# Last weight block cut 448+64 instead of 384+64x2, its wide store issued by ScalarE, engine programs run in two visits

## The reference

```python
fl = _ln(xf, pn_g, pn_b)
pf = _merge(attention(fl, Wqk_p, Wv_p) + conv) @ Wout_p
wv = _heads(_ln(xw, wn_g, wn_b) @ Wv_w)      # [4, 16384] @ [16384, 1024]
wf = nds @ wv + conv(wv)
wf = _merge(wf) @ Wout_w                     # [4, 1024] @ [1024, 16384]
out = wfeat + wf                             # back to the image
return out + x
```

## Time and profile before

| | us |
|---|---|
| median of 3 runs | 747.84 |
| the profiled execution's own time | 747.63 |
| its span, first to last instruction | 746.40 |
| around the span | 1.23 |
| DMA queue 1 busy | 99.5% of 16 engines' span |
| PE busy (matmul) | 436.4, 58% |
| DVE, ACT, POOL busy | 91.5, 38.2, 9.3 |
| granted TensorE clock, mean | 0.78 |

### The profile page before, as it was taken

The page is one execution under the profiler, slowest core; times in us unless marked ns, Lnnn a source line. Parts: engine busy times, 40 slices in busy tenths (PEclk is TensorE's granted clock), DMA queues, the critical chain, the costliest instruction groups (busy, mean ns, idle before and its releaser), DMA issues.

```text
span 746.4 us, 6667 instructions
## 1 busy us (share of the span) xinstructions
PE 436.4 (58%) x2895; PEld 129.9 (17%) x2895; DVE 91.5 (12%) x254; ACT 38.2 (5%) x80; POOL 9.3 (1%) x21
## 2 busy tenths in 40 slices
PE   7699944444445454454586989445444454544548
PEld 5333200000001111111122332000000011111113
DVE  2765200000002000000005161000000020000000
ACT  2211100000000000000001111000000000000000
POOL 2100000000000000000001000000000000000000
PEclk9689977777767777777788899876776777777779
DMA  9999999999999999999999999999999999999998
GB/s 394 447 394 436 454 415 439 436 443 418 436 446 418 439 433 443 421 432 446 418 439 436 417 434 443 446 418 432 443 432 432 432 446 418 432 443 432 432 415 347
DMA packets 7923, 320.45 MB, mean 429 GB/s; under 512 B 1049, under 2 KB 1585, under 8 KB 2153
## 3 DMA queue, kind: packets, MB, share of 16 engines
q1 hardware_dynamic: 7913, 320.31, 99.5%
HBM read 319.82 MB, written 0.49 MB: 429 GB/s over the span
## 4 chain that ended last, share of the span: by engine, by line
DMA 64%; PE 32%; DVE 3%; ACT 1%; issue 0%; SPq 0%; DVEq 0%; ACTq 0%
DMA ring<-halves 60%; PE bank L485 10%; PE bank L512 9%; PE bank L404 4%; DMA ring<-last 4%; PE bank L421 2%; PE bank L413 2%; PE bank L536 1%; PE bank L341 1%; PE bank L323 0%; PE bank L389 0%; DMA cst<-blurs 0%; DVE ring L722 0%; PE bank L381 0%; PE bank L354 0%
## 5 line engine op out<-in xcount | busy, mean ns | idle before, releaser
L485 PE MATMUL bank<-ring,stage 128*4 128x512 f32 x1024 | 141.4, 714 | 141.1 <-DMA ring<-halves 141.1
L512 PE MATMUL bank<-ring,wf_t 128*32 128x512 f32 x960 | 137.9, 739 | 127.3 <-DMA ring<-halves 127.3
L512 PEld LDWEIGHTS bank<-ring,wf_t 128*32 128x32 f32 x960 | 33.7, 133 | 221.1 <-DMA ring<-halves 121.0
L485 PEld LDWEIGHTS bank<-ring,stage 128*4 128x4 f32 x1024 | 27.0, 97 | 255.1 <-DMA ring<-halves 154.1
L932 DVE TENSOR_TENSOR image<-bank,image 128x32 f32 (+1 forms) x30 | 5.1, 193 | 277.6 <-PE bank L323 277.6
L897 DVE COPY wv_t<-bank 128x32 f32<-128x32 f32 x2 | 0.4, 192 | 287.1 <-PE bank L323 287.1
L323 PE MATMUL bank<-ident,area 128*128 128x128 f32 (+1 forms) x117 | 18.3, 284 | 12.3 <-ACT area L653 11.1
L653 ACT COPY area<-bank 128x512 f32<-128x512 f32 x15 | 8.8, 586 | 281.2 <-PE bank L512 281.2
L404 PE MATMUL bank<-extra,area 128*64 128x512 f32 x64 | 18.2, 734 | 3.3 <-DVE area L806 3.3
L469 PE MATMUL bank<-extra,area 128*64 128x512 f32 x64 | 17.6, 712 | 2.0 <-DVE area L871 2.0
L323 PEld LDWEIGHTS bank<-ident,area 128*128 128x128 f32 (+1 forms) x117 | 12.5, 141 | 30.9 <-ACT area L653 23.8
(11 more groups left out here) (208 smaller groups left out, 217.0 us busy)
## 6 DMA issues: line engine op xcount, KB each, us to landing
extra<-ends SPq DMA_DIRECT2D x4, 4096.0 KB, 16.0
ring<-halves SPq DMA_DIRECT2D x4, 4096.0 KB, 20.3
ring<-last SPq DMA_DIRECT2D x1, 3072.0 KB, 22.1
ring<-last SPq DMA_DIRECT2D x2, 1536.0 KB, 25.5
ring<-last SPq DMA_DIRECT2D x1, 1024.0 KB, 28.6
ring<-last SPq DMA_DIRECT2D x1, 768.0 KB, 29.6
ring<-halves SPq DMA_DIRECT2D x33, 29.4
ring<-images SPq DMA_DIRECT2D x1, 512.0 KB, 3.6
```

What stands on the lines that cost most here:

```text
L485: m = mm(bank[0][32 * j:32 * j + 4, :], stage[:, k // 8, at:at + 4], w[:, j], start=False, stop=False)
L512: m = mm(bank[6 + g][32 * j:32 * j + 32, :], wf_t[:, h, :], w[:, j], start=(h == 0), stop=(h == GROUP - 1))
```

## The change

1. WIDE becomes 448: the wide pieces hold heads 0 to 3, 4 to 6 and 7, the narrow ones (64 columns) heads 0 to 4, 5 to 6 and 7. The loads are six as before, of the same bytes in sum.
2. The wide columns' store is issued by ACT, right behind its copy and a wait for its own semaphore; SP no longer waits for the copy.
3. The written-out group of the last half but one goes back into the loop over the turns, whose second part is now under an If; so its turn_group stands ahead of piece 0.
4. The residual is added by full-width matmuls (128 stationary columns): three of 128 moving columns and, for the block that is split, two of 64.
5. The programs of PE, ACT and DVE are each wrapped in a loop of two visits. In the first, every part is skipped; in the second, it runs. DVE's body is cut into two functions, `first` with `layer(0)`, and `layer(1)`, each under an If.

```diff
-WIDE = 384
-LAST_PIECES = ((0, WIDE, 0, 4), (0, WIDE, 4, 6), (0, WIDE, 6, 8), (WIDE, BANK, 0, 4), (WIDE, BANK, 4, 7), (WIDE, BANK, 7, 8))
+WIDE = 448
+LAST_PIECES = ((0, WIDE, 0, 4), (0, WIDE, 4, 7), (0, WIDE, 7, 8), (WIDE, BANK, 0, 5), (WIDE, BANK, 5, 7), (WIDE, BANK, 7, 8))
...
@@ sync
-            sp.wait_ge(wide_copied, 1)
-            sp.dma_start(windows_last[:, 0:WIDE], area[5][:, 0:WIDE]).then_inc(rows_stored, 16)
             sp.wait_ge(last_copied, 1)
...
@@ tensor
+            with pe.Fori(0, 2) as visit:
+                with pe.If(visit > 0):
+                    pe.wait_ge(blurs_landed, 16)
...
-                with pe.Fori(0, TURNS - L) as i:
-                    for g in range(2):
-                        group(L, i, g)
-                        turn_group(i * 2 + (2 * TURNS * L + g + 1), g)
+                        with pe.Fori(0, TURNS) as i:
+                            group(L, i, 0)
+                            turn_group(i * 2 + (2 * TURNS * L + 1), 0)
+                            with pe.If(i + L < TURNS):
+                                group(L, i, 1)
+                                turn_group(i * 2 + (2 * TURNS * L + 2), 1)
...
-            group(1, TURNS - 1, 0)
             last_piece(0)
-            turn_group(4 * TURNS - 1, 0)
             last_piece(1)
...
             for s8 in range(4):
-                for j in range(4):
-                    if s8 < 3:
-                        mm(bank[7][32 * j:32 * j + 32, s8 * P:s8 * P + P], residual[:, s8, j, :], ident, start=False, stop=False)
-                    else:
-                        mm(bank[6][32 * j:32 * j + 32, 0:P], residual[:, s8, j, :], ident, start=True, stop=False)
+                n = min(P, WIDE - s8 * P)
+                mm(bank[7][:, s8 * P:s8 * P + n], residual[:, s8].rearrange("p j w -> p (j w)"), ident[:, 0:n], start=False, stop=False)
+                if n < P:
+                    mm(bank[6][:, 0:P - n], residual[:, s8].rearrange("p j w -> p (j w)"), ident[:, n:P], start=True, stop=False)
...
@@ scalar
+            with act.Fori(0, 2) as visit:
+                with act.If(visit > 0):
+                    act.wait_ge(pads_zeroed, 1)
...
+                    sc.copy(area[5][:, 0:WIDE], bank[7][:, 0:WIDE]).then_inc(wide_copied, 1)
+                    act.wait_ge(wide_copied, 1)
+                    sc.dma_start(windows_last[:, 0:WIDE], area[5][:, 0:WIDE]).then_inc(rows_stored, 16)
...
@@ vector
+            with dve.Fori(0, 2) as visit:
+                with dve.If(visit > 0):
+                    first()
+                    layer(0)
+                with dve.If(visit > 0):
+                    layer(1)
```

More of the change, by code:

```diff
@@ L335, in first_there @@
                     half_there(L, None, s // HALF)
[L338 to L371, removed]
@@ L723, in _, with first @@
[L723 to L732 removed]
+            def first():
+                dve.wait_ge(images_landed, 16)
+                v.tensor_tensor(l0_sq[:, :, :], l0_in[:, :, :], l0_in[:, :, :], ALU.mult).then_inc(squared, 1)
+                dve.wait_ge(blurs_landed, 16)
+                v.tensor_tensor(blocks_x[:, :, :].rearrange("p b (x c) -> p (b x) c", c=C), cc("taps_x").unsqueeze(2).to_broadcast([P, 5 * XM, C]),
+                                cc("same_c").unsqueeze(1).to_broadcast([P, 5 * XM, C]), ALU.mult).then_inc(blocks_built, 1)
+                dve.wait_ge(blurred_y2, 1)
+                v.tensor_copy(l0_blur[:, 1, BANK:2 * BANK], bank[3][:, :]).then_inc(blur2_copied, 1)
+                mean_c = area[6][:, :]
+                dve.wait_ge(mean_sq, 1)
+                then(v.tensor_copy(mean_c, bank[5][:, :]))
+                for i, (sq, fields) in enumerate(((7, 2), (0, 4))):
+                    dve.wait_ge(field_ready, fields)
+                    dve.wait_ge(mean_sq, i + 1)
+                    then(v.tensor_tensor(l0_part[:, i], bank[sq][:, :], l0_part[:, i], ALU.subtract))
+                    v.tensor_scalar(l0_part[:, i], l0_part[:, i], 0.0, None, ALU.max).then_inc(l0_var, 1)
+                    if i == 0:
+                        dve.wait_ge(l0_std, 1)
+                        then(v.tensor_scalar(l0_part[:, 0], l0_part[:, 0], EPS, None, ALU.add))
+                        then(v.reciprocal(l0_part[:, 0], l0_part[:, 0]))
+                work = l0_blur[:, 0, 0:BANK]
+                dve.wait_ge(field_ready, 5)
+                then(v.tensor_tensor(work, bank[4][:, :], mean_c, ALU.subtract))
+                then(v.tensor_tensor(work, work, l0_part[:, 0], ALU.mult))
+                dve.wait_ge(l0_std, 2)
+                then(v.scalar_tensor_tensor(work, l0_part[:, 1], EPS, work, ALU.add, ALU.mult))
+                dve.wait_ge(pads_zeroed, 1)
+                v.tensor_tensor(pixels.rearrange("p y x -> p x y"), work.rearrange("p (x y) -> p x y", y=IMG),
+                                bank[6][:, :].rearrange("p (x y) -> p x y", y=IMG), ALU.add).then_inc(image_ready, 1)
@@ L766, in softmax, with layer @@
                 return v.tensor_tensor(x, x, wide(2), ALU.mult)
-            for L in range(2):
+            def layer(L):
                 vv = vec[:, L, :]
```

503 lines of the change are left out of this document (252 added, 251 removed).

## The result

The changed kernel takes a median of **749.84 us** (9 runs, 749.30 to 750.55), the kernel before 747.84 (9 runs, 747.60 to 748.36): a ratio of 1.0027, interval 1.0018 to 1.0036. That is 2.0 us more, slower by 0.27%, and the whole interval lies above 1. The forecast was 748.8 in a range of 747.3 to 750.0: the time lies in the range, but above the forecast's own spread (748.0 to 749.3), and the sum missed it by a microsecond, as much as the whole effect that it forecast. The profiled execution took 749.64 us, with a span of 748.4; its predicted span was 747.46.

The account below looks back on a forecast made before the run. Loading bounds the kernel, one queue busy 99.5% of the span. PE's work after piece 1's later landing adds 1.06 us, giving a 747.46 span; plus 1.23 gives 748.69, stated as 748.8 us, range 747.3 to 750.0.

Parts of the forecast that it names:

- the forecast's own spread: Total time: 748.0 to 749.3 us if PE is late by about a microsecond; chance 0.66.
- The landings of the last block: Wout's last block: piece 1 seen at 739.3 us, piece 2 at 741.4, the last at 743.9 as before.
- After piece 1: Tail from 739.34 us: PE's remaining work is all on the path, DVE's copy at 745.63, span 747.46, +1.06 us.
- Full-width residual: Tail, residual on PE: 10 full-width instructions take 1.04 us against 0.90 for 32 tiled ones; nothing won.
- ACT's store: Tail, wide columns: issued at 745.30 us, lands at 747.27, 0.2 us ahead of the narrow store, so hidden.
- turn_group ahead of piece 0: Before piece 1: piece 0 starts by 735.0 us, takes 3.0, ready at 738.0, leaving 1.3 us of wait.
- Two-pass programs: Start of the kernel: the first visit costs between nothing and some code loads, hidden by waits and 8.4 us slack; taken as nothing.
- The last load lands at 743.9 whatever happens: End of the load stream: last landing fixed at 743.9 us, so a time below 746.3 was given only 0.03.
- 1 (narrow matmuls no faster): Narrow pieces in the tail: 64 columns run at the 128-column pace, chain grows by 0.86, 749.6 us; chance 0.12.
- 2: End of the tail: ACT's store ends last, up to 1 us more, 748.9 to 749.7 us; chance 0.09.
- 3: Tail stays the DMA's: PE meets piece 5 at 743.94 us and waits for it, time 747.3; chance 0.08.
- 4: Queue dry where layer 1 begins, or clock falling ahead of piece 1: 750 to 754 us; chance 0.05.

Follow-up runs that it names:

- one visit: The changed kernel with the programs of PE, ACT and DVE run once, without their two-visit loops: 748.88 us, ratio 1.0016 to the kernel before.

## Why the prediction missed by a microsecond

- **The landings of the last block**: right. Piece 1 was to be seen at 739.3, and is at 739.23 where the visits are absent; 0.86 later where they are not.
- **After piece 1**: right term by term. Forecast: piece 1 with its gap 2.36, rows 1.02, residual 1.04, piece 2 and the narrow pieces 0.75 + 1.12 = 1.87. Measured: 2.46, 1.02, 0.84 + 0.22 = 1.06, 1.83. The 448-wide pace of 0.376 per four instructions was 0.376. Measured by itself, this part cost 1.08 us where +1.06 was forecast. That DVE's copy came at 745.63 to the hundredth is luck in part: piece 1 was seen 0.11 earlier than the sum's 739.34 and took 0.10 longer.
- **Full-width residual**: right that it wins nothing: 1.06 us for 10 instructions against 0.90 for 32.
- **ACT's store**: right. Issued at 745.29 in "one visit" where 745.30 was forecast, and worth nothing by the run with SP's.
- **turn_group ahead of piece 0**: piece 0 was to start by 735.0 and starts at 735.52 without the visits, 735.89 with them; the trace has 0.46 and 0.68 us of "issue" there, at the branches out of the folded loop, and piece 0 took 3.21 where 3.0 was forecast. I had said that 1.3 us of wait ahead of piece 1 cover it, and they do (0.49 and 0.99 us of PE's idle time are left over).
- **Two-pass programs, "I take nothing, up or down"**: this is the step that failed. It cost 1.08 us, as much as all the rest. The reasoning was that PE waits for its blurs until 4.74 anyhow, and that 8.4 us of slack in the queue come after. Both are true, and the slack was never used up in the changed kernel. But slack protects the stream from a late *engine*; it doesn't protect it from being late *itself*. The visits' fetches touch the first loads and SP's issue of them, at a point where the queue has no work in store, and a stream that is busy 99.5% of the time makes up for little of it: 0.4 of 1.3 us. "The last load lands at 743.9 whatever happens" fell with it: 0.87 us of the miss are seen in the chain before the last block has begun.
- Of the bounds I had named for this step, "nothing" and "some code loads", I took the lower one because the page's total of 7 packets is 0.1% of the DMA time. The total was the wrong row: what mattered was when the packets come.
- **The range**: that 749.84 lies in it is luck. Its part above 749.3 was there for narrow matmuls, ACT's store and a dry queue or a fallen clock, and none of these happened; the visits, which did bring the time there, were put at nothing.

**Rivals.** 1 (narrow matmuls no faster) fell: 64 instructions of 64 columns passed in 0.9 us, as this line of the changed kernel shows for their weights:

```profile
745.35 0.91 PEld L558 LDWEIGHTS bank<-ring,wf_t 128*32 128x32 f32 x60 [0.25 <-issue]
```

That is 15 ns each, 0.06 per four, and the 64 matmuls keep that pace: four start 7 ns apart, and the next four 56 ns after the first ones. The floor of about 25 ns that the Trainium skill states (TensorE: Matmul & The Clock Gate, Back-to-back issue gap) doesn't hold for these 32-column tiles side by side. 2 fell with the run of SP's store. 3 fell: no wait for a load behind piece 1. 4 did not happen in the changed kernel, whose queue never ran dry, but its mark, Wout's blocks later than 704.94, did; the mark couldn't tell a dry queue from a late one. A queue drained to its last 1.2 us came only in the run with the visits held back. The other half of 4, a clock that falls in PE's wait ahead of piece 1, didn't happen either: the granted clock of the changed kernel is 1.00 from 740.0 to 746.4 us.

## What to carry to other kernels

Where one DMA queue is busy from the first microseconds to the last, slack shown between a load's issue and its landing covers late engines only; whatever touches the start of the stream (the issuer, the first loads, code fetched beside them) is for the greater part still there at the end, here 0.87 of 1.28 us. Before costing a change of control flow at nothing, look up not how many instruction packets there are, but when they come and what they come beside. And when a wait for data is to be removed, ask first how long the engine's own chain behind it is, at the clock that is granted after the wait: here it was as long as the wait it would have saved.

## What the runs showed of the hardware

- Jumps over whole programs before the first load has landed bring instruction packets forward (two of queue 8 with PE's, two and one of queue 14 with DVE's and ACT's, between 3 and 12 us, none before), and cost a saturated stream about 1 us for three engines (1.28 at the first half's landing, 0.87 at Wout's).
- With PE's jumps, one issue of SP took 1.27 to 1.60 us instead of 0.44, and ended 0.36 us after PE's first code packet of 16 KB, in six kernels of six. With DVE's or ACT's, SP's issues stay as they were and the first 8.39 MB load takes 0.6 to 0.8 us longer.
- The same jumps, made once the queue is full of weights, keep PE from its first matmul for 7.59 us, where ahead of the loads it was 0.95.
- Four 32-column tiles side by side are no slower than full-width matmuls: the same residual took 0.90 us as 32 tiled instructions and 1.06 us as 10 full-width ones. With 64 moving columns four tiled matmuls start every 56 ns.
- After its long wait for the last whole half PE did the first 3.7 us (in another kernel 4.9 us) of its work at 1.2 GHz; the two groups of the same 64 instructions took 8.96 and 9.56 us.
